# First-pass matmuls of the attention loop issued in pairs, with the step's other ring work behind them

## The reference

```python
qk = (x @ Wqk_w.T + Wqk_b).reshape(b, n, H, E, 2)         # x: (2, 1024, 512), H = E = 8
scores = jnp.einsum('bhqd,bhkd->bhqk', q, k)
attn = jax.nn.softmax(scores, axis=-1) / HEAD_DIM ** 0.5
out = jnp.einsum('bhsl,bhlv->bhsv', attn, v)              # then @ Wo_w.T + Wo_b
x = _layernorm(x + attention(x))
x = _layernorm(x + down(silu(gate(x)) * up(x)))           # 512 -> 1792 -> 512
```

## Time and profile before

| what | value |
|---|---|
| three runs | 571.86, 572.08 and 576.48 us; median 572.08 us |
| profiled execution | 576.28 us, its span 574.5 us, mean granted TensorE clock 0.968 |
| PE, DVE, ACT, POOL busy | 531.3, 422.3, 406.5, 234.2 us |
| attention loop | 62.2 to about 259 us of the span |

### The profile page before, as it was taken

The page is one execution under the profiler, slowest core; times in us unless marked ns, Lnnn a source line. Parts: engine busy times, 40 slices in busy tenths (PEclk is TensorE's granted clock), DMA queues, the critical chain, the costliest instruction groups (busy, mean ns, idle before and its releaser), DMA issues.

```text
span 574.5 us, 7484 instructions
## 1 busy us (share of the span) xinstructions
PE 531.3 (92%) x2640; PEld 198.7 (35%) x2640; DVE 422.3 (74%) x725; ACT 406.5 (71%) x579; POOL 234.2 (41%) x267
## 2 busy tenths in 40 slices
PE   9897888989889989989999999999999999999992
PEld 3222212222122212214444445444454444544441
DVE  3589796978898799244877678766688667787666
ACT  1430675757677768997788877878878887787881
POOL 8020740002291255263546332673334733338442
PEclk9899597979999999999999999999999999999998
DMA  5593175002231003021004000010000010000101
GB/s 174 160 192 66 40 138 181 1 2 57 91 37 39 3 0 76 2 47 28 1 1 56 18 2 0 2 63 12 0 2 1 0 74 0 2 1 1 73 2 73
DMA packets 29237, 24.59 MB, mean 43 GB/s; under 512 B 19632, under 2 KB 21552, under 8 KB 29200
## 3 DMA queue, kind: packets, MB, share of 16 engines
q1 hardware_dynamic: 25328, 17.56, 11.4%
q0 software_dynamic: 3872, 6.56, 5.9%
HBM read 20.08 MB, written 4.19 MB: 42 GB/s over the span
## 4 chain that ended last, share of the span: by engine, by line
PE 72%; DVE 19%; ACT 3%; issue 2%; DMA 2%; SPq 1%; POOL 0%; POOLq 0%; ACTq 0%; DVEq 0%
PE ps L842 17%; PE ps L854 17%; PE ps L871 16%; DVE mxh L971 14%; PE ps L793 5%; PE ps L726 5%; PE ps L760 3%; PE ps L666 3%; PE ps L778 2%; PE ps L712 2%; ACT pbuf L557 1%; DMA stack<-mp 1%; SPq L335 1%; PE ps L880 1%; DVE st L1010 1%
## 5 line engine op out<-in xcount | busy, mean ns | idle before, releaser
L971 DVE TENSOR_REDUCE mxh<-ps 128x1 f32<-128x512 f32 x256 | 162.1, 682 | 28.4 <-PE ps L726 26.9
L1092 DVE TENSOR_SCALAR ps<-ps,ratio 128x512 f32<-128x512 f32 x168 | 121.8, 755 | 80.9 <-PE ps L854 80.5
L557 ACT ACTIVATE pbuf<-ps,gamma 128x1024 f32<-128x1024 f32 x128 | 135.2, 1115 | 49.7 <-PE ps L778 49.3
L612 ACT ACTIVATE ps<-ps,ratio 128x512 f32<-128x512 f32 x168 | 106.0, 657 | 41.7 <-PE ps L842 41.7
L871 PE MATMUL ps<-stack,wd 128*128 128x512 f16 x448 | 129.5, 379 | 0.6 <-POOL stack L484 0.6
L842 PE MATMUL ps<-arena,wg 128*128 128x512 f16 x448 | 115.3, 379 | 0.1
L854 PE MATMUL ps<-arena,wu 128*128 128x512 f16 x448 | 115.3, 379 | 0.0
L633 ACT ACTIVATE ps<-ps,ratio 128x512 f32<-128x512 f32 x156 | 102.7, 664 | 16.4 <-PE ps L871 16.4
L726 PE MATMUL ps<-stack 64*128 64x512 f16 x256 | 89.6, 407 | 13.6 <-DVE mxh L971 9.3
L482 POOL CAST stack<-pbuf 128x512 f16<-128x512 f32 x56 | 34.1, 609 | 141.3 <-DVE pbuf L1099 141.3
L793 PE MATMUL ps<-pbuf,arena 128*32 128x512 f32 x512 | 71.2, 629 | 0.6 <-ACT pbuf L557 0.6
(11 more groups left out here) (100 smaller groups left out, 330.5 us busy)
## 6 DMA issues: line engine op xcount, KB each, us to landing
arena<-xT SPq DMA_DIRECT2D x16, 256.0 KB, 5.6
x<-x SPq DMA_DIRECT2D x2, 2048.0 KB, 10.1
out<-x SPq DMA_DIRECT2D x3, 1024.0 KB, 4.2
wg<-gq POOLq DMA_DIRECT2D x4, 448.0 KB, 10.3
wu<-uq POOLq DMA_DIRECT2D x4, 448.0 KB, 12.7
wd<-dq POOLq DMA_DIRECT2D x2, 896.0 KB, 10.7
out<-x SPq DMA_DIRECT2D x4, 256.0 KB, 2.4
stack<-mp SPq DMA_DIRECT2D x48, 2.0 KB
```

Of the source, the lines that this page charges most:

```text
L557: nc.scalar.activation(pbuf[:, pi % 4, :].rearrange("p (a n) -> p a n", a=2), ps[:, 2 * (pi % 2):2 * (pi % 2) + 2, :], ACT.Exp, scale=gamm ...
L612: nc.scalar.activation(gbank[t % 2], gbank[t % 2], ACT.Copy, scale=gr[:, t % G, c:c + 1])\
L971: nc.vector.tensor_reduce(mxh[:, f % 2, qh, half:half + 1], ring_bank("first", n, 0), AX.X, ALU.max)\
L1092: nc.vector.tensor_scalar(ubank[t % 2], ubank[t % 2], ur[:, t % G, c:c + 1], None, ALU.mult)\
```

## The change

In `ring_at`, f2 and f3 are put ahead of the step's other use instead of behind it. In PE's loop, f0 and f1 are issued together behind the first score pair, and everything else, f2, f3 and then M, avT, attT or wo, stands between the second score pair and `av(n-1)`. Nothing is left for the place behind `av`. No instruction is added or taken away.

```diff
@@ ring_at(n)
-            return first[0:2] + other + first[2:4]
+            return first + other
@@ PE's loop over the steps
                 uses = ring_at(n)
-                late = max(1, len(uses) - (2 if len(uses) >= 4 else 0))
+                early = 2 if uses and uses[0][0] == "first" else 0
                 scores(n, 0)
-                for use in uses[0:1]:
+                for use in uses[0:early]:
                     ring_use(*use)
                 scores(n, 1)
-                for use in uses[1:late + 1]:
+                for use in uses[early:]:
                     ring_use(*use)
                 if n:
                     av(n - 1)
-                for use in uses[late + 1:]:
-                    ring_use(*use)
             av(ALL - 1)
```

## The result

The changed kernel is slower: 588.34 us median (587.37 to 590.17, four runs) against 572.14 us, a ratio of 1.027 with a 95% interval of 1.021 to 1.032. The forecast was 583.5 us, from 576 to 590, slower by over 1% with a chance of 0.78. The sign, the place and the mechanism were right. The sum, 11.4 us, fell short of the 16.2 us between the medians. Some executions of either order, the profiled ones of "f1 alone" and of "the new places with the ring order of before" among them, spend longer at 1.2 GHz and take over 1.5% longer than the fastest; ratios and medians of the experiments leave them out, and of those two profiles only lengths of steps are used.

What follows compares the result with a forecast made beforehand. PE and DVE waiting for each other over three banks, a 2.48 us loop per step, was taken as the bound. Terms 2.2 + 4.0 + 2.0 + 0.4 + 1.9 + 0.5 + 1.5 - 1.1 = +11.4 us gave 583.5 us, range 576 to 590.

Steps and rivals of the forecast that it cites:

- The loop of waits: Attention loop: r0, f3, `av`, score pair, f0, r0 takes 2.71 us per plain step against 2.48; wo steps 4.05 against 3.54.
- The DMAs behind M: Steps 16, 32 and 48: M's later split makes scores wait for its DMAs, +1.9 us (bounds 0 and 2.7).
- The busy stretches: Steps 25 to 31 and 41 to 47, DVE nearly full: its idle time grows, +0.5 us (bounds 0 and 2).
- step 52: Step with f0, f1 and a wo no longer ahead of anything in the loop: about -0.5 us.
- M's own term: M steps 13, 21 and 37, DVE the bound in both kernels: +0.2, 0.1 and 0.1, together +0.4 us.
- Steps 9, 17 and 18 lie in stretches that wait for something else: nothing: These avT or attT steps were put at no added time, as their stretches wait for something else.
- The start: Up to step 8: 1.0 of 2.3 us for M's later split and landing, 0.5 for step 8; +1.5 us.
- The end: Step 52 about -0.5 us; steps 54 to 56, ACT the bound, -0.2 each; together -1.1 us.
- The pairing pays: Rival: f0 and f1 share one PE pass, eight wo steps gain 0.5 us each, 567 us; chance 6%.
- Other waits absorb it: Rival: stalls at 8 and 17, unmoved DMA landing and DVE-bound stretches absorb additions, 575 to 578 us; chance 14%.
- The clock falls more often: Rival: longer PE gaps at steps 27 and 43 bring 1.2 GHz, 2.5 us each time, 588.5 us; chance 16%.
- in another place: Sign of being wrong, whole kernel: the granted clock falls in another place; no size given.

Runs made afterwards that it cites:

- f1 alone: Kernel before with f0 and f1 issued together behind the first score pair, f3 still behind `av`, ring order as before; ratio 1.000 to the kernel before.
- the new places with the ring order of before: Changed kernel's places on PE, but ring order f0, f1, the other use, f2, f3; ratio 1.011 to the kernel before.
- second profiles: Kernel before and changed kernel profiled again with no edit; 570.64 and 588.00 us.
- halved reductions: Both kernels with first-pass reductions over 256 of the 512 columns; 554.29 us for the kernel before, 571.16 us for the changed one, one run each.
- M back between f1 and f2: Changed kernel with M alone put back between f1 and f2 in the ring; 585.66 us, ratio 1.019 to the kernel before.
- two kernels without the stalls: Both kernels with down-weight loads issued after step 8's first scores and `scale_ratios` moved from step 16 to 58; 564.70 us before, 581.76 us changed.

## Why the prediction was right, and where its size fell short

The same steps compared in the second profiles of both kernels, and in the first ones (us; the forecast's terms sorted by step):

| steps | forecast | second profiles | first profiles |
|---|---|---|---|
| 2 to 8 | +1.5 | +2.68 | +0.90 |
| 9 | 0 | +0.58 | -0.05 |
| 10 to 16 | +1.8 | +1.68 | +1.68 |
| 17 and 18 | 0 | +2.05 | -0.25 |
| 19 to 24 | +2.3 | +2.20 | +1.91 |
| 25 to 31 | +0.25 | +0.23 | +0.23 |
| 32 | +0.7 | +0.72 | +2.81 |
| 33 to 40 | +3.3 | +3.16 | +4.09 |
| 41 to 47 | +0.25 | +0.21 | +0.21 |
| 48 | +1.1 | +1.22 | +1.09 |
| 49 to 51 | +1.2 | +1.11 | +1.13 |
| 52 and 53 | -0.5 | -0.52 | -0.52 |
| 54 to the end | -0.6 | +0.27 | +0.26 |
| sum | +11.4 | +15.6 | +13.5 |

(Roundings leave 0.1.) The rest of the 17.4 us between the second profiles, 1.8, lies ahead of the first `av`; between the first ones it is 0.4. Where the two columns differ, one of the four profiles has a stretch at the half clock that its partner has not, or the long wait at step 32; the rows where they agree show the change alone.

- **The loop of waits, right.** Plain steps 2.70 us (2.71 forecast), wo steps 4.04 (4.05), avT and attT steps 3.57 (3.59). Shown by "f1 alone", which leaves f3 in its place and loses nothing, and by the halved reductions, which shorten both loops by 0.27 and keep the 0.22 between them.
- **The DMAs behind M, right in place and size:** 0.5, 0.5 and 1.1 us in steps 16, 32 and 48 above what "M back between f1 and f2" has there. The wait of over 2 us at step 32, in two of four profiles with the late M, was in no term; its cause is open.
- **The busy stretches and step 52, right; M's own term, +0.4, too high:** step 13 with its successor takes 6.16 us against 6.06, so 0.1, and 21 with 22 and 37 with 38 lose no more than a wo step's 0.5.
- **"Steps 9, 17 and 18 lie in stretches that wait for something else: nothing", wrong.** This is the term that was mis-sized most: 2.6 us by the second profiles. A stall ahead of a step does not shorten the loop behind it. All three hold an avT or attT and cost 0.5 us each like the others: step 17 went from 5.62 to 6.25 with the stall nearly unchanged (PE waits 2.48 and 2.58 us). In the two kernels without the stalls they have 3.09, 3.09 and 3.08 against 3.57, 3.57 and 3.55, 1.4 us in all. The other part is a stretch at 1.2 GHz from 121.9 us on. Both profiles of the changed kernel have it, and the kernel before had one twice as long in its first profile and none in its second, which is why the first profiles show no loss there.
- **The start, +1.5, not settled within its bounds of 0 to 2.8:** 2.68 us by the second profiles, 0.90 by the first. 1.08 of the 2.68 is step 2, at the half clock in both profiles of the changed kernel and in the first of the kernel before (3.79 us there, 2.92 in the second). The landing did move: counted from the first `av`, the six DMAs are issued 1.2 us later between the first profiles and 2.2 between the second, and the scores of step 8 start 0.8 and 1.65 us later, where the forecast took 1.0 of 2.3. With the other load out of the way that wait is gone before and 0.4 us after, as at step 16.
- **The end: -1.1 forecast, -0.25 measured.** Step 52 gave its 0.5, but that ACT is the bound in steps 54 to 56 did not carry a gain of 0.6: PE goes through these steps of the kernel before without a wait too. ACT's exponentials did fall from 2.32 to 2.12 us, but steps 55 and 56 only from 2.70 to 2.59, which is what PE's own path takes now. And step 54 rose from 2.70 to 3.24: its second score pair waits 0.47 us for an exponential, and the wo, which stood between the two pairs, now waits with it. Step 54 on PE, second profile of the changed kernel:

```profile
247.86 0.39 PE L778 MATMUL ps<-stack 64*128 64x512 f16 x2 [0.47 <-ACT pbuf L557]
248.18 1.13 PE L760 MATMUL ps<-wo_s,attT 96*128 96x512 f32 x2
249.24 1.07 PE L793 MATMUL ps<-pbuf,arena 128*32 128x512 f32 x8
```

- **The rivals.** "The pairing pays" fell: f0 and f1 do share a pass, and "f1 alone" gains nothing by it. "Other waits absorb it" fell by the table. "The clock falls more often" came only in part. No profile of the changed kernel has a fall behind step 27 or 43, where it was expected. The falls are at steps 2, 8 and 17 and, in the first profile, at 32 behind the long wait, where step 33 takes 4.51 us instead of 3.57: that is "in another place", one of the prediction's own signs of being wrong. That 588.34 us is nearly the number this rival gave (588.5) is luck.

TensorEngine Tiling (Array Packing), in the Trainium skill, warns under "Gotcha 1: PSUM Pressure" that different row tiles write to different banks. The trace agrees, with f3 waiting 0.35 us in a plain step for the bank of its own step's f0.

## What to carry to other kernels

When two engines pass banks of a small ring to and fro, find the loop of waits in one step, and ask of every instruction whether it is inside or outside of it. An edit that leaves the work alone can still move something into the loop; here the score pair's pass of 0.22 us, and with the wo a second reduction. And a step that begins with a long stall still has its own length behind it: a stall hides only what runs beside it.

## What the runs showed of the hardware that was not expected

A gap of PE does not decide alone whether the granted clock falls. Behind `scale_ratios` PE waited for 2.48 us in both profiles of the kernel before. In the first the clock then was 0.50 for 6.82 us; in the second it stayed at full speed over the same steps:

```profile
115.62 0.39 PE L726 MATMUL ps<-stack 64*128 64x512 f16 x1 [2.48 <-DVE mxh L971]
```

In the changed kernel the gap there is 2.58 us, and the clock fell behind it in both profiles. The gap of 1.63 us at step 27 of the changed order was followed by a fall in the changed kernel without the stalls, and by none in the first profile of the changed kernel.

The mean granted clock of an execution goes with its time: it was 0.978 to 0.984 in the executions of the kernel before that took 570.4 to 572.8 us, and 0.967 or 0.968 in those of 576.2 to 576.8. With the two long stalls taken out of the kernel before, its five runs lay within 0.9 us (564.30 to 565.14). The same edit left the changed kernel's runs 4 us apart (580.43 to 584.50), so the two stalls are not all of the scatter.
